# SyncE's queue in a new order, x turned one iteration earlier, and the router's logits behind the attended values

## What is computed

```python
# q from layernorm(x), k = v = ctx; 16 heads of 16, causal
x = x + tanh(g_xattn) * attention(layernorm(x), ctx, ctx)
# router: softmax(xn @ w_router + b_router), the top 4 of 16 blocks are kept
mask = top_k(softmax(xn @ w_router + b_router), 4)
h = relu(einsum('nd,ebd->neb', xn, w1) + b1)           # xn = layernorm(x), 16 blocks of 64
x = x + tanh(g_ffn) * (einsum('neb,ebd,ne->nd', h, w2, mask) + b2)
```

## Time and profile before

| | |
|---|---|
| runs shown | 699.85, 701.86, 703.02 us; median 701.86 |
| profiled execution, own time | 705.3 us |
| its span, first to last instruction | 703.5 us |
| mean granted TensorE clock | 0.995 |
| PE busy | 661.8 us (94%) |
| POOL busy | 553.7 us (79%) |
| ACT busy | 542.1 us (77%) |
| DVE busy | 527.3 us (75%) |
| share of the 16 DMA engines taken by SP's and ACT's DMAs | 47.3% |

### The profile page before, as it was taken

One profiled execution on the slowest core, in us unless ns is written; L12 is line 12 of the kernel. 1 busy time (PEld: TensorE's weight loads), 2 busy tenths in 40 slices (PEclk: granted clock), 3 DMA queues, 4 the chain that ended last, 5 costly groups with the idle time before them and its releaser, 6 DMA issues.

```text
span 703.5 us, 30579 instructions
## 1 busy us (share of the span) xinstructions
PE 661.8 (94%) x12960; PEld 612.6 (87%) x12960; DVE 527.3 (75%) x1429; ACT 542.1 (77%) x785; POOL 553.7 (79%) x718
## 2 busy tenths in 40 slices
PE   5778999999999999999999999999999999999998
PEld 4667889889989898999899988999998988899997
DVE  5698877777777777787687777777877778777752
ACT  4577787888888788888788778888987878887742
POOL 6577778779878788888888877988897888787742
PEclk9899999999999999999999999999999999999999
DMA  6232365764446667445635547646544665452111
GB/s 182 70 83 50 74 119 108 101 119 101 89 118 126 94 108 123 68 119 126 113 89 126 87 101 122 124 85 119 122 88 100 126 98 104 96 94 52 42 30 39
DMA packets 192279, 69.24 MB, mean 98 GB/s; under 512 B 166160, under 2 KB 191888, under 8 KB 192144
## 3 DMA queue, kind: packets, MB, share of 16 engines
q1 hardware_dynamic: 191312, 65.72, 47.3%
q10 hardware_dynamic: 832, 1.57, 0.7%
HBM read 19.03 MB, written 8.39 MB: 39 GB/s over the span
## 4 chain that ended last, share of the span: by engine, by line
PE 36%; SPq 21%; DMA 14%; DVE 11%; issue 8%; POOL 8%; ACT 2%; POOLq 0%; DVEq 0%
PE score_banks L344 6%; DMA qT<-qT 6%; SPq L980 5%; SPq L990 5%; PE bank L423 4%; SPq L1017 4%; PE bank L425 3%; PE bank L424 3%; PE bank L446 3%; PE bank L447 3%; PE bank L448 3%; DMA xT_parts<-xn_parts 3%; POOL q_parts L857 3%; PE bank L357 3%; SPq L1009 3%
## 5 line engine op out<-in xcount | busy, mean ns | idle before, releaser
L880 POOL TENSOR_TENSOR h_low<-hid,h_high 128x512 fp32r<-128x512 f32 x128 | 164.1, 1282 | 12.6 <-ACT hid L560 12.5
L873 POOL TENSOR_SCALAR_AFFINE_SELECT weights<-weights 128x1024 f32<-128x1024 f32 x128 | 138.2, 1103 | 39.4 <-ACT weights L525 37.2
L738 DVE SCALAR_TENSOR_TENSOR hid<-bank,b_cols,used_all 128x256 f32<-128x256 f32 x248 | 108.3, 478 | 77.9 <-PE bank L425 47.5
L525 ACT ACTIVATE weights<-score_banks 128x1024 f32<-128x1024 f32 x128 | 124.3, 1024 | 41.1 <-PE score_banks L344 40.9
L423 PE MATMUL bank<-xT_high,w_high 128*128 128x256 f32 x496 | 151.5, 305 | 0.4 <-DVE hid L738 0.4
L425 PE MATMUL bank<-xT_high,w_low 128*128 128x256 f32 x496 | 139.5, 281 | 0.0
L424 PE MATMUL bank<-xT_low,w_high 128*128 128x256 f32 x496 | 139.2, 281 | 0.0
L446 PE MATMUL bank<-w_high,h_high 128*128 128x256 f32 x488 | 137.3, 281 | 0.7 <-POOL h_low L880 0.7
L447 PE MATMUL bank<-w_low,h_high 128*128 128x256 f32 x488 | 137.7, 282 | 0.0
L448 PE MATMUL bank<-w_high,h_low 128*128 128x256 f32 x488 | 136.3, 279 | 0.0
L423 PEld LDWEIGHTS bank<-xT_high,w_high 128*128 128x128 f32 x496 | 93.3, 188 | 8.3 <-DVE hid L738 0.7
(11 more groups left out here) (105 smaller groups left out, 1405.8 us busy)
## 6 DMA issues: line engine op xcount, KB each, us to landing
x_in<-in_x SPq DMA_DIRECT2D x31, 256.0 KB, 4.2
out_y<-y_out SPq DMA_DIRECT2D x31, 256.0 KB, 2.5
c_in<-in_ctx SPq DMA_DIRECT2D x30, 256.0 KB
qT<-qT SPq DMA_DIRECT2D x128, 4.0 KB
w_stage<-in_w1T ACTq DMA_DIRECT2D x1, 1024.0 KB, 5.9
hid<-in_w2T SPq DMA_DIRECT2D x8, 128.0 KB, 2.6
kT_parts<-k_parts SPq DMA_TRANSPOSE x57
qT_parts<-q_parts SPq DMA_TRANSPOSE x57, 2.8
```

What stands on the lines that cost most here:

```text
L525: act.activation(weights[:, b % 2, half * 2 * HB:(half + 1) * 2 * HB, :].rearrange("p h q -> p (h q)"), score_banks[:, 2 * half:2 * half + ...
L738: dve.scalar_tensor_tensor(hid[:, n % 4, j], hid_bank(n)[:, j * TOKS:(j + 1) * TOKS], b1_cols[:, c:c + 1], used_all[:, p % 2], ALU.add, AL ...
L873: pool.affine_select(out=w, in_=w, compare_op=ALU.is_ge, fill=0.0, base=0, pattern=[[0, 2 * HB], [1, S]], channel_multiplier=-1).then_inc( ...
L880: pool.tensor_tensor(h_low[:, p % 2, chunks], hid[:, n % 4], h_high[:, p % 2, chunks].bitcast(F32), ALU.subtract).then_inc(h_low_made, 1)
```

## The change

Three edits of order; no arithmetic is changed, and every instruction keeps its size.

1. SP: x is turned in iteration i for tile i-2 instead of i-3 (that is, one iteration earlier), and stands behind the q transpose. The row of maxima thus follows `used` at once. The loads (even i) and the store (odd i) stand right behind the row of maxima, ahead of the q transpose. The load of x runs 8 tiles ahead and that of c 4 tiles ahead, where both ran 6 ahead; each with its own condition.
2. POOL: `x_split(i-2)` stands ahead of `values` and `key_parts`.
3. PE and ACT, even iterations: attention_out(i-1) and its copy stand ahead of the router's logits and their copy.

```diff
-LOAD_AHEAD = 6
+X_AHEAD, C_AHEAD = 8, 4
@@ tensor
+                if 0 <= i - 1 < N:
+                    attention_out(i - 1)
                 if pr is not None:
                     router_logits(pr, i)
-                if 0 <= i - 1 < N:
-                    attention_out(i - 1)
@@ scalar
+                if 0 <= i - 1 < N:
+                    out_copied(i - 1)
                 if pr is not None:
                     act.wait_ge(routed, pr + 1)
...
-                if 0 <= i - 1 < N:
-                    out_copied(i - 1)
@@ gpsimd
+                if 0 <= i - 2 < N and not x_by_pe(i - 2):
+                    x_split(i - 2)
                 if i == FIRST:
                     values(0)
...
-                if 0 <= i - 2 < N and not x_by_pe(i - 2):
-                    x_split(i - 2)
@@ sync
             for i in ITERATIONS:
                 pu = used_pair(i)
-                if 0 <= i - 3 < N and not x_by_pe(i - 3):
-                    x_turned_by_dma(i - 3)
                 if pu is not None:
                     used_spread(pu)
                 if 0 <= i < N:
                     max_row(i)
+                if i % PAIR == 0:
+                    if 2 * PAIR <= i + C_AHEAD < N:
+                        load_context(i + C_AHEAD)
+                    if 2 * PAIR <= i + X_AHEAD < N:
+                        load_x(i + X_AHEAD)
+                if 0 <= i - OUT_LAG - 1 < N:
+                    store(i - OUT_LAG - 1)
                 if QUERIES_BY_PE <= i + 3 < N + MAX_LAG:
                     queries_spread(i + 3)
+                if 0 <= i - 2 < N and not x_by_pe(i - 2):
+                    x_turned_by_dma(i - 2)
                 if KEYS_BY_PE <= i + 3 < N:
                     keys_spread(i + 3)
```

More of the change, by code:

```diff
@@ L950, in _, with load_context, load_x @@
         def _(sync):
[L951 to L957, removed]
-                sync.dma_start(c_in[:, cs * PAIR:(cs + 1) * PAIR, :],
-                               A_ctx[tiles].rearrange("b p d -> p b d")).then_inc(c_landed[cs], 16)
-                if n * PAIR >= XS:
-                    sync.wait_ge(x2_made, n * PAIR - XS + PAIR)
+            def load_context(b):
+                cs = b // PAIR % (CS // PAIR)
+                sync.wait_ge(v_made, b - CS + PAIR)
+                if b - CS + PAIR > KEYS_BY_PE:
+                    sync.wait_ge(k_parts_made, b - CS + PAIR - KEYS_BY_PE)
+                sync.dma_start(c_in[:, cs * PAIR:(cs + 1) * PAIR, :],
+                               A_ctx[b:b + PAIR].rearrange("b p d -> p b d")).then_inc(c_landed[cs], 16)
+            def load_x(b):
+                xs = b // PAIR % (XS // PAIR)
+                if b >= XS:
+                    sync.wait_ge(x2_made, b - XS + PAIR)
                 sync.dma_start(x_in[:, xs * PAIR:(xs + 1) * PAIR, :],
-                               A_x[tiles].rearrange("b p d -> p b d")).then_inc(x_landed[xs], 16)
+                               A_x[b:b + PAIR].rearrange("b p d -> p b d")).then_inc(x_landed[xs], 16)
             def max_row(b):
@@ L1018, in x_turned_by_dma, with store @@
                                          xn_parts[:, slot].rearrange("p l d -> p (l d)")).then_inc(x_spread[slot], 16)
+            def store(b):
+                n, t = divmod(b, PAIR)
+                if b < N - PAIR and t == PAIR - 1:
+                    sync.wait_ge(y_made, b + 1)
+                    sync.dma_start(out[b - 1:b + 1].rearrange("b p d -> p b d"), y_out[:, n % 2]).then_inc(y_stored[n % 2], 16)
+                elif b >= N - PAIR:
+                    sync.wait_ge(y_made, b + 1)
+                    sync.dma_start(out[b], y_out[:, n % 2, t]).then_inc(y_stored[n % 2], 16)
             for i in ITERATIONS:
                 pu = used_pair(i)
-                if 0 <= i - 3 < N and not x_by_pe(i - 3):
-                    x_turned_by_dma(i - 3)
                 if pu is not None:
@@ L1039, in _ @@
                                        allow_slow_non_contiguous=True).then_inc(b1_landed, 16)
[L1040 to L1050, removed]
             for n, stored in enumerate(y_stored):
```

## The result

The changed kernel takes 681.28 us, the median of 4 runs (680.42 to 682.85), against 700.96 us of the kernel before in the same comparison (699.85 to 703.02): a ratio of 0.9719, 95% interval 0.9687 to 0.975. The forecast was 681.0. The profiled execution took 680.97 us, with a span of 679.1.

A forecast was written before the change was run, and what follows sets the result against it. PE's own queue was taken as the bound, 10.03 us per iteration, with 20.7 us above it; 13.8 + 5.9 + 2.8 - 1.5 = 21.0 us off the 701.86 median gave 681 us, 8-in-10 range 676 to 692.

The forecast's parts named there:

- The bound and its size: Steady part: PE's own queue sets a floor of 10.03 us per iteration, so the change can give 20.7 us at most.
- The row of maxima, 13.8 us: SP, odd iterations: row issued 1.7 us earlier, so all 13.8 us of PE's waits ahead of shifted_scores go.
- x turned earlier, 5.9 us: x issued an iteration earlier: ACT's wait for x goes, and PE's 5.9 us ahead of the router's logits.
- POOL's order, 0: POOL's x_split ahead of values and key_parts: cost 0, up to 0.1 us per pair.
- k one transpose later, 0: Keys turned 1.25 us later on SP, but ACT joins them only in the next iteration, behind q: cost 0.
- PE's and ACT's order, 0: Router's logits behind attended values, same 24 matmuls: gain or loss within 0.3 us per pair, taken as 0.
- The start, 2.8 us: x loaded right behind router's weights: DVE's 3.95 us wait nearly gone, PE starts earlier; 2.8 us, bounds 0 and 4.5.
- The bound of 1.7 to 3.0 us from the row of maxima: Start: tile 0's row of maxima lands at 15.1 to 16.4, so PE starts 1.7 to 3.0 us earlier.
- What comes back, 1.5 us: Even iterations: late q transposes delay the next row of maxima; 1.5 us lost again in all, bounds 0 and 8.
- No change, or a mere renaming: Rival: ACT's join holds the row of maxima, so the wait only changes its name; about 700 us, chance 0.08.
- Part of it comes back: Rival: q late by 2.5 us in most even iterations, 11 us lost again; about 692 us, chance 0.16.
- Slower through q behind the loads: Rival: even iterations' q transpose, some 3 us behind 512 KB of loads, lands 3.4 us late; about 712 us, chance 0.06.

The follow-up runs named there:

- e10: Kernel before with one SP edit: loads (x 8 ahead, c 4 ahead) and store moved into the gap behind the row of maxima; 682.37 us, 0.9722.
- e4: Changed kernel with the loads (x 8 ahead, c 6 ahead) and the store back at the end of SP's iteration; 719.34 us, 1.0223.
- e5: Changed kernel with POOL's order as before (x split behind values and keys); 683.57 us, 0.9744.
- e1: SP's new order and look-ahead alone, with POOL's, PE's and ACT's order as in the kernel before; 693.66 us, 0.9868.
- e9: Changed kernel with PE's and ACT's order as before (router ahead of the attended values); 688.56 us, 0.9804.
- e7: Changed kernel with two more unused 256 KB loads in each even iteration from 8 to 58, behind the two in the gap; 685.3 us, 0.975.
- e3: Kernel before with one SP edit: x transpose of tile i-3 behind the row of maxima, not turned an iteration earlier; 764.3 us, 1.0794.
- e6: Kernel before with only the start changed: x of tiles 4 to 7 loaded right behind the router's weights; 701.43 us, 0.9984.
- e8: Changed kernel, x of tiles 4, 5 loaded ahead of gates, biases and router's weights, tiles 6, 7 behind first row of maxima; 684.18 us, 0.9731.
- e12: Changed kernel with k ahead of x on SP, POOL's order as before, and the start of e8; 682.84 us, 0.9715.

## Why the prediction was right, step by step

- **The bound and its size: right.** PE's floor of 10.03 us and the 20.7 us above it were the right frame. 19.7 were recovered, and the floor didn't move.
- **The row of maxima, 13.8 us: right in size, wrong in part in its cause.** I counted c, x's load and the x transpose, 2.41 us, as taken from its way. The x transpose isn't: it stands between q and the row in both kernels. What is taken away are the two loads, 341.32 - 340.20 = 1.12 us of issuing (1.13 at the median of all odd iterations, not the 1.7 that I took), and with them what they do to the landing. e10, which moves the loads alone, has the same ratio (0.9722); e4, which turns x early and leaves the loads, is 2.2% slower than before.
- **x turned earlier, 5.9 us: the wait went, but the step named was not needed for it.** The early turn alone is enough (e4: no wait for x, with the loads at their old place), and so is moving the loads alone: in e10 x is turned at its old place and PE's wait ahead of the router is 0.6 us. x had been late because it went out directly behind the loads.
- **POOL's order, 0: right beside PE's new order** (e5); beside the old one it is open (e1 and e9).
- **k one transpose later, 0, and PE's and ACT's order, 0: both wrong singly, right in their sum.** I wrote that ACT joins k only in the next iteration, and looked no further. k makes ACT late by up to 1.8 us, x behind it in ACT's queue too, and PE waits for that x: 8.7 us in e1. The new order on PE covers it: e9 against the changed kernel, 0.9804 against 0.9719, some 6 us. These two zeros were a cost and a cover of about the same size; that they cancel was luck. The counts of 16 and 24 matmuls given with this edit are wrong too: in the traces the attended values are 32 matmuls (1.08 us) and the router's logits 8 (0.43 us). Nothing in the sum used them.
- **The start, 2.8 us: 2.95 to the first exponential** (20.26 by 17.31), in part by the clock, and another wait took DVE's place: DVE still waited 1.27 us for x (I had said under 1), and PE 2.28 us for the row of maxima (timelines of DVE and PE, changed kernel):

```profile
12.56 0.43 DVE L645 BATCH_NORM_STATS2 stats<-x_in 128x6 f32<-128x256 f32 x1 [1.27 <-DMA x_in<-in_x]
```
```profile
16.07 1.17 PE L344 MATMUL score_banks<-qT,kT 32*128 32x128 f32 x32 [2.28 <-DMA qT<-qT]
```

The load took 7.1 us to land, longer than the 6.2 that bounded it; the 1 MB load of w1 was on its way with it. The bound of 1.7 to 3.0 us from the row of maxima held: 18.12 - 16.07 = 2.05, and shifted_scores itself took 1.17 instead of 2.09, with a granted clock of 0.76 from 17 to 24 us against 0.51. So 2.05 of the 2.95 us are an earlier start and most of the rest is the clock.
- **What comes back, 1.5 us:** less; from 60 to 640 us 1.9 us of PE's waits are left in all, of which 1.0 (DVE's maxima of an early tile) is not new. The difference of the two profiled executions, 705.3 - 680.97 = 24.3, is above my sum of 21.0; the medians differ by 19.7 (interval of the ratio: 17.5 to 21.9). The profiled execution of the kernel before was one of the long ones; its runs scatter more than those of the changed kernel, perhaps since its waits hang on landings, which no run tests.
- **The number itself, 681.0 against 681.28: closer than the reasoning deserves.** The gain between the medians was 1.3 us smaller than my 21.0, and the kernel before had a median of 700.96 in the comparison where I had subtracted from 701.86. The two offsets nearly cancel.
- **The rivals.** No change, or a mere renaming: no. Part of it comes back: it does, in e1 and e9, through k and x and not through q, as I had it. Slower through q behind the loads: e7 shows the cover at twice the loads. Slower is what e3 is, through x, and e4, through the row of maxima.

## What to carry to other kernels

When a transfer is late, list what its queue issues between the event that releases the chain and that transfer, and ask of each item whether the change really takes it out from between; an item moved to another place in between is still in the way. Large loads that nobody awaits soon belong in a gap where the queue waits anyway, since they delay what is issued behind them both in issuing and in landing. And an edit whose worth alone cannot be told can be the cover for what another edit makes late: cost each edit with the others in place, following the late item through the in-order queue of the engine that receives it.

## What the runs showed of the hardware

- What follows a load directly pays for it. In the kernel before, the x transpose issued at 341.32, right behind both loads, was awaited by ACT until 346.6, 5.3 us on. In 23 iterations from 60 to 640 us in which ACT waited for such an x, the wait ended 4.8 us after the issue at the median (4.1 to 5.9). The x transposes behind the store of an odd iteration landed after 2.6 us at the median there (longest 4.7). q, issued some 3 us behind the loads, kept a median of 2.7 in the changed kernel (longest 4.9).
- Issuing a DMA transpose occupied SP 1.2 to 1.3 us as a rule, but single issues took up to 2.5 (x) and 2.8 us (k) before and up to 2.8 (x) after, without a cause that the profile shows. Such an issue is up to 1.6 us longer than the others, more than the slack near 1 us of the row of maxima; what they cost was not separated. After the change PE had no wait for a DMA from 60 to 640 us.
- At the start, where PE has gaps, the granted clock falls to its level of 1.2 GHz for a while, at places that differ from kernel to kernel: 17 to 24 us before (0.51) and in the changed kernel in part (0.76), not at all in that stretch in e6 (1.00), 31 to 38 us in e8 (0.77). In e12, whose edits of the start are those of e8, it is 0.82 from 5 to 12 us instead, and the first exponential starts at 18.37 us where e8 has 16.90. The difference is as large as what the edits of the start themselves give, so from one profile each neither the total nor the first exponential's time can judge them to better than some 1.5 us.
